# Splitting one projection of eight matmuls around the transposes of the probabilities in a grouped-attention stage

## The reference, cut to what matters

```python
q = _fp8_linear_pertensor(ln_out, wq, wq_scale, q_in_scale).reshape(b, s, g, hpg, d)
q = _ln(q, qln_w, qln_b)
k = _ln(_fp8_linear_pertensor(ln_out, wk, ...).reshape(b, s, g, d), kln_w, kln_b)
v = _fp8_linear_pertensor(ln_out, wv, ...).reshape(b, s, g, d)
core = _gqa(q, k, v).reshape(b, s, nh * d)
qx = _ln(_fp8_linear_pertensor(ln_out, wqx, ...).reshape(b, s, g, hpg, d), qxln_w, qxln_b)
kvx = jnp.einsum('bsi,oi->bso', cond, w_kv_x)
...
xout = _gqa(qx, kx, vx).reshape(b, s, nh * d)
catq = _div_clamp_fp8(jnp.concatenate([core, xout], axis=-1), proj_smooth)
return jnp.einsum('bsi,oi->bso', catq, wproj) * (proj_in_scale * proj_w_scale)
```

## Time and profile before

| what | us |
|---|---|
| median of three runs | 2093.26 |
| lowest and highest | 2092.05, 2093.97 |
| the profiled execution | 2092.42 |
| its span, from the first instruction to the last | 2090.6 |
| TensorE busy in the span | 2021.3 (97%) |
| VectorE, ScalarE, GpSimd busy | 1412.0, 1243.6, 667.7 |
| grouped attention, step 2 to step 58 | 237.1 to 1036.9 in the span |

### The profile page before, as it was taken

How to read it: one execution, slowest core, us unless ns; L and a number is a source line. 1 busy time by engine, 2 the same in 40 slices (tenths; PEclk the granted TensorE clock), 3 DMA queues, 4 the chain that set the end, 5 groups by cost and what they waited for, 6 DMA issues and landing times. The chain is left out here.

```text
span 2090.6 us, 31900 instructions
## 1 busy us (share of the span) xinstructions
PE 2021.3 (97%) x11332; PEld 1579.3 (76%) x11352; DVE 1412.0 (68%) x3113; ACT 1243.6 (59%) x3195; POOL 667.7 (32%) x637
## 2 busy tenths in 40 slices
PE   8999899999999999999998999999999999998998
PEld 5644778888888888888886886665666785666997
DVE  2397576777777777767667747667677658885555
ACT  2073787888787878788774445553554346772332
POOL 1300354444445354535430002324341101222442
PEclk9999999999999999999999999999999999999999
DMA  4033433243424242432222204313322220003200
GB/s 184 22 119 110 134 117 115 73 143 87 146 74 142 87 138 78 128 102 88 92 95 101 76 3 159 132 58 126 116 105 113 86 74 19 2 2 120 107 1 32
DMA packets 60176, 193.71 MB, mean 93 GB/s; under 512 B 9409, under 2 KB 28641, under 8 KB 56049
## 3 DMA queue, kind: packets, MB, share of 16 engines
q1 hardware_dynamic: 48498, 172.16, 24.6%
q10 hardware_dynamic: 9504, 8.50, 1.4%
q0 software_dynamic: 2016, 11.01, 1.3%
HBM read 171.75 MB, written 19.49 MB: 91 GB/s over the span
## 5 line engine op out<-in xcount | busy, mean ns | idle before, releaser
L985 PE MATMUL psum<-la_w_both,context 128*128 128x256 f32 (+1 forms) x1536 | 343.9, 380 | 0.0
L985 PEld LDWEIGHTS psum<-la_w_both,context 128*128 128x128 f32 (+1 forms) x1536 | 277.6, 184 | 44.9
L1456 POOL TENSOR_TENSOR norm_std<-room 128x400 f32<-128x400 f32 x75 | 70.3, 938 | 337.8 <-DVE room L1221 337.7
L942 PE MATMUL psum<-qa_xqf,qa_two 128*128 128x400 f32 x640 | 142.1, 365 | 2.4 <-PEq L60 2.4
L3026 ACT ACTIVATE it_prob<-psum,it_nm 100x257 f32<-100x257 f32 (+1 forms) x256 | 101.9, 413 | 40.0 <-DVE it_nm L3057 39.9
L942 PEld LDWEIGHTS psum<-qa_xqf,qa_two 128*128 128x128 f32 x640 | 119.3, 191 | 7.5 <-issue 3.2
L1003 PE MATMUL psum<-qa_kxT,room 128*100 128x361 f32 x256 | 102.5, 482 | 2.5 <-issue 1.1
L1449 POOL TENSOR_TENSOR room<-room,qa_inv 128x500 f32<-128x500 f32 x64 | 82.1, 1283 | 55.0 <-DMA qa_inv<-qa_std_rows 50.9
L1817 PE MATMUL psum<-gf_parts,gf_w 128*128 128x400 f32 x480 | 93.0, 346 | 0.0
L2565 POOL TENSOR_TENSOR gf_last_diff<-la_gf_what,la_gf_w 128x512 bf16<-128x512 bf16 x24 | 27.0, 1146 | 206.4 <-issue 170.2
L1146 ACT ACT_TABLE_LOAD x64 | 82.1, 1283 | 13.5 <-ACT qa_size L1166 7.1
(11 more groups left out here) (400 smaller groups left out, 5315.5 us busy)
## 6 DMA issues: line engine op xcount, KB each, us to landing
context<-in_context SPq DMA_DIRECT2D x70, 722.0 KB, 5.3
qa_inv<-qa_std_rows SPq DMA_DIRECT2D x64, 250.0 KB, 4.1
qa_w_raw<-in_qa_w SPq DMA_DIRECT2D x8, 1536.0 KB, 16.1
la_gf_raw<-in_gf_w SPq DMA_DIRECT2D x16, 768.0 KB, 4.7
qa_piece<-in_tf_pieces ACTq DMA_DIRECT2D x64, 128.0 KB, 2.1
la_w_qt<-in_qa_o SPq DMA_DIRECT2D x8, 1024.0 KB, 5.5
gf_ternary<-la_gf_made POOLq DMA_DIRECT2D x7, 768.0 KB
gf_ternary<-keep POOLq DMA_DIRECT2D x7, 768.0 KB
```

What stands on the lines that cost most here:

```text
L942: mm = pe.matmul(psum[:, bank, 0:HALF], two[:, part, j, k, :], xqf[:, PART_XQ[j], k, (h % 2) * HALF:(h % 2 + 1) * HALF], start=(k == 0 and ...
L985: mm = pe.matmul(psum[0:rows, i // 2, (i % 2) * 256:(i % 2) * 256 + 256], ctxT[:, n % 2, k, t0:t0 + rows], kv_raw[:, s, k, :], start=(k == ...
```

## The change

In every step from 1 on the `behind` head's eight matmuls are cut in two: the first two chunks of the width (four matmuls) stay ahead of `turn_probs`, the last two (four matmuls) stand behind it. The accumulation in bank 2 of PSUM stays open across the transposes, which write banks 6 and 7. `unit_mm` is raised by the last of the eight, so it comes after the transposes. Step 0 and the `ahead` heads stay as they were. No instruction is added or removed on any engine; VectorE, ScalarE, GpSimd and SyncE keep their order.

```diff
-            def project_unit(u):
+            def project_unit(u, chunks=range(C)):
 
                 h, j = half_and_part(u)
                 bank = bank_of(u)
-                if h >= 2:
-                    pe.wait_ge(S_["w_lo"], (h // 2 - 1) * PARTS + j + 1)
-                if u >= len(FIRST):
-                    pe.wait_ge(S_["raw_ready"], u - 1 if u <= len(FIRST) + 1 else u)
-                for k in range(C):
+                if chunks[0] == 0:
+                    if h >= 2:
+                        pe.wait_ge(S_["w_lo"], (h // 2 - 1) * PARTS + j + 1)
+                    if u >= len(FIRST):
+                        pe.wait_ge(S_["raw_ready"], u - 1 if u <= len(FIRST) + 1 else u)
+                for k in chunks:
                     for part in range(2):
                         mm = pe.matmul(psum[:, bank, 0:HALF], two[:, part, j, k, :],
                                        xqf[:, PART_XQ[j], k, (h % 2) * HALF:(h % 2 + 1) * HALF],
                                        start=(k == 0 and part == 0), stop=(k == C - 1 and part == 1))
-                mm.then_inc(S_["unit_mm"], 1)
+                if chunks[-1] == C - 1:
+                    mm.then_inc(S_["unit_mm"], 1)
...
                 project_context(g, s, b, n)
+                around = n
                 for u in behind(n):
-                    project_unit(u)
+                    project_unit(u, range(C // 2) if around else range(C))
                 if not early(n, 1):
                     turn_probs(n - 1)
+                for u in behind(n) if around else ():
+                    project_unit(u, range(C // 2, C))
                 if not early(n, OUT_LAG):
                     project_out(*out_chunk(g, b, n))
```

## The result

The changed kernel takes 2080.76 us (median of six runs, beside 2093.61 us for the kernel before); the ratio is 0.9941, with a 95% interval of 0.9929 to 0.9952. It is faster by 0.5 to 0.7%. One of its six runs took 2204.71 us at a mean granted clock of 0.927 where the others have 0.991 to 0.994, and one of the six of the kernel before took 2131.85 us; the ratio leaves such slow runs out.

A forecast was written before the change was run, and what follows sets the result against it. TensorE looked saturated but hid short waits at step heads, caused by late transposes. Terms -9.4 - 3.0 + 4.4 + 2.8 - 2.0 = -7.2 us took the median from 2093.26 to 2086.0 us; range 2082 to 2093.5 us.

The forecast's parts named there:

- (a): Steps with n mod 4 = 0 or 1, from 8: earlier transposes give back 0.36 us in 26 steps, -9.4 us.
- The scores need s + 1.53 less two matmuls of 0.18, s + 1.16: Within (a), s being a step's start: earliest start of the scores, reckoned from step 31, which has two more L955 matmuls.
- Their own head gains nothing, as in step 31: Said in (c) of steps with n mod 8 = 3: the start of these steps gets no shorter.
- (c): Steps with n mod 8 = 3, 11 to 51: transposes wait for L1318, +0.73 us in six steps, +4.4 us.
- The chain and its slack: Head chain from the transposes comes 0.71 us earlier; probabilities still in time by 0.13 us after the 0.05.
- Rival 2: ScalarE cannot get ahead, so transposes wait in steps with n mod 8 = 1, 4, 5: 2092.6 us; chance 0.20.
- (b): Steps with n mod 4 = 2, 10 to 58: only 0.23 us ahead of L955 comes back, 13 steps, -3.0 us.
- (d): Steps with n mod 8 = 6: 0.30 us becomes wait, half of 0.23 us lost to GpSimd's L1468; +2.8 us.
- (e): Steps 1, 2, 4, 5, without output projection: matmuls fill L1022's wait, 4 x 0.5 us, -2.0 us.
- Rival 1: VectorE's copy L1221 waits for the raw head's second half: slower, +6.2 us, 2099.5 us; chance 0.10.
- Rival 3: (d) costs nothing because the meeting with L1468 falls out well: -10.0 us, 2083.3 us; chance 0.08.

The follow-up runs named there:

- eight behind: Changed kernel with all eight matmuls of the raw head behind the transposes instead of four: 2102.11 us, ratio 1.0041 to the kernel before.
- late measurement: Changed kernel with ScalarE's measurement of the weights moved behind the exponentials where n mod 8 = 3: 2073.32 us, ratio 0.9905 to the kernel before.

## Why the prediction was right in direction and wrong in size

**What bounds the kernel: right.** TensorE is 97% busy before and after, and yet the stage lost 13.0 us of waits on balance: what it won came at the heads of steps and, in the four early ones, ahead of L1022, and what it paid came ahead of the transposes.

**(a), the term that was mis-sized.** Forecast 0.36 us in 26 steps, measured 0.49: 3.4 of the 5.8 us by which the sum was off. The step that failed is "The scores need s + 1.53 less two matmuls of 0.18, s + 1.16". It took step 31 for a step whose scores wait for nothing. They did wait. In the kernel before, step 31's turned keys end at 646.07 (645.43 and 0.64) and its scores start 0.10 us later, at 646.17, the same distance as in step 36, 715.94 to 716.03:

```profile
645.43 0.64 ACT L1140 ACTIVATE qa_kxT<-psum,params 128x361 f32<-128x361 f32 x1
```

In the changed kernel they end 0.60 us ahead of the scores, which now start at s + 1.45 behind four L957 (638.02 to 639.47):

```profile
638.22 0.65 ACT L1145 ACTIVATE qa_kxT<-psum,params 128x361 f32<-128x361 f32 x1
...
639.47 0.77 PE L1005 MATMUL psum<-qa_kxT,room 128*100 128x361 f32 x2
```

From s + 1.45, two matmuls of 0.18 less give s + 1.09, which is what step 36 does. That is 0.08 of the missing 0.13 us; the other 0.05 us is the longer first pair of a start out of a wait (0.66 and 0.61 us). The run with two matmuls behind has a wait of both parts still in it, and takes 13.3 us.

**"Their own head gains nothing, as in step 31": wrong for the same reason.** Steps with n mod 8 = 7 gained 0.14 us each, 1.0 us, with the same two parts (in step 31 the scores start 0.08 us earlier, and the first pair takes 0.60 us instead of 0.66). In those with n mod 8 = 3 the gain is hidden in the wait of (c).

**The chain and its slack: right.** The turned keys, the low part of the head, the wait of 0.72 us and that of 0.51 us went as foretold. The probabilities were to end 0.18 us ahead of the transposes, 0.13 after the 0.05 of the shortest way. L1323 ends at 715.70, s + 8.47, and the transposes start at 715.83, s + 8.60: 0.13 us, so 0.08 was left. Rival 2, in which they come too late, did not happen in these steps; eight behind shows what it costs when they are late.

**(b): right,** 0.26 us for the 0.23 of the forecast.

**(c): right,** 0.72 us for 0.73. The late measurement then showed whose wait it is: ScalarE's order. The cut only made the transposes reach it 0.73 us earlier.

**(d): too dear by 0.8 us** (with the (b) of the same steps +1.4 forecast, +0.6 measured). The normalisation that met GpSimd's work in the earlier trace rows meets it again and takes the same 1.17 us, but GpSimd's work came earlier too (it ends at s + 9.68 instead of s + 9.98), so that the half that I set down for the meeting was not lost:

```profile
741.93 1.32 POOL L1473 TENSOR_TENSOR qa_v<-qa_w_raw,qa_v 128x512 bf16<-128x512 f32 x1
...
742.15 1.17 DVE L1323 TENSOR_SCALAR qa_prob<-qa_prob,qa_rsum 100x100 f32<-100x100 f32 x1
```

My premise that GpSimd's work stays where it is was wrong. GpSimd is dense from its L1485 to this instruction (L1480 and L1468 before), and ahead of L1485 it waits 0.50 us for VectorE's L1351 (L1346 before). That started at s + 2.68 in the kernel before (744.54) and starts at s + 2.39 in the changed one (735.96), and the whole row came 0.3 us forward in the step. L1323 ends at 743.32, 0.07 us after GpSimd's 743.25, as before (751.91 and 751.84); by the rule of the Trainium skill that I named (SBUF — State Buffer, section "SBUF: two separate sides") that is what a locked port pair looks like, and the trace agrees again. The meeting that did change is another. Of the six steps from 14 on, step 46 took 15.29 us instead of 14.93, in all three executions that have this cut there. There VectorE's clip of the step's outputs (L1346 of the changed kernel) starts 0.05 us behind GpSimd's L1479 and takes 1.48 us; in step 38 it starts 0.17 us ahead of it and takes 0.36 (the instruction behind it on VectorE then takes 1.24):

```profile
734.28 0.36 DVE L1346 TENSOR_SCALAR qa_yb<-la_w_kt 128x400 bf16<-128x400 f32 x1
734.45 1.36 POOL L1479 TENSOR_TENSOR qa_o<-la_w_qt,qa_o 128x512 fp32r<-128x512 f32 x1 [0.77 <-DVE qa_o L1282]
...
844.93 1.29 POOL L1479 TENSOR_TENSOR qa_o<-la_w_qt,qa_o 128x512 fp32r<-128x512 f32 x1 [0.78 <-DVE qa_o L1282]
844.98 1.48 DVE L1346 TENSOR_SCALAR qa_yb<-la_w_kt 128x400 bf16<-128x400 f32 x1
```

What follows on both engines is 0.35 us later in step 46, and so are its transposes. Why the clip starts 0.21 us later there than in the other steps is not shown. Without this one step, (d) was too dear by 1.2 us.

**(e): right in sum,** 2.2 us for 2.0, with some luck: the four steps gave 0.52, 0.74, 0.32 and 0.65 us where I had set down 0.5 for each.

**Rival 1** did not happen. Its cover of 0.15 us was real, and the run with the second half behind the output projection shows the loss behind it, +12.9 us against the kernel before rather than the 6.2 that I gave it; that run delays the head by a whole output projection, which is more than the rival supposed. **Rival 3**, at 2083.3 us, was nearest to the result, but by its (d) alone it explains 0.8 of the 5.8 us.

The range failed with the term: I had put the ends of the unknown costs into (c), (d) and the rivals, and none on (a), since I took its 0.36 us for a measured figure. It was worked out from two steps, and the scores waited in both.

## What to carry to other kernels

Before a step without waits is used as the yardstick for one with waits, look at what releases its own first instructions: here every start of the scores 0.10 us behind the end of ScalarE's keys was a wait, even in step 31, where TensorE was busy for all of its 13.69 us. Where a matmul group has to make room for transposes, count both sides for each kind of step, how much earlier the chain behind the transposes comes and how long the transposes' own operand is already there; here 0.13 us between ready probabilities and their transposes was all that stood between a gain of 0.49 us and a wait. And where the consumer's engine waits while its next operand lies ready, as VectorE did here, changing that engine's order can give most of the gain (here 0.43 of 0.49 us in three of four kinds) without a wait ahead of the transposes.

## What was not expected of the hardware

A start out of a wait costs TensorE more than the wait. The first two matmuls of the scores (L1003, 128x361 f32, one in the code) take 0.66 us up to the first L1004 where they had waited, and 0.61 us in the changed kernel, where they had not; step 31 shows 0.66 and 0.60. The twelve profiled executions agree by kinds of steps: 0.66 us wherever the scores start 0.10 us behind the end of the keys, 0.60 to 0.61 wherever the distance is larger.

The granted clock differs between executions of one program, in places that have nothing to do with the change. The stage won 13.0 us between steps 1 and 60, and the profiled span shows 11.2. Step 1 started 0.5 us later than before, since step 0 began at 207.17 instead of 206.56 (in another execution of the changed kernel at 207.68), and the part behind step 60 took 1.4 us more, though no instruction in it differs. In both profiled executions TensorE had half the full clock (0.50, which is 1.2 GHz) in several short stretches, but not the same ones. The changed kernel had one of 6.8 us just behind the stage, where the kernel before had one of 3.4 us, and one of 3.4 us from 1590.1 on, where the kernel before had none. The window of the first, and that of the kernel before in the same place:

```profile
1095.20:1102.00 6.80, 6.36 (x14) 4.71 (x15) 1.77 (x6) 0.06 (x1) 1.45 (x2) 0.50 0.00 0
...
1107.90:1111.30 3.40, 3.08 (x9) 3.11 (x10) 0.21 (x2) 0.00 (x0) 0.00 (x0) 0.50 0.00 0
```

In the first, eight matmuls of L173 take 4.62 us:

```profile
1098.44 4.62 PE L173 MATMUL psum<-X,avg 128*128 128x400 f32 x8
```

Another profiled execution of the same program gave them 3.00 us, and had the full clock where the second stretch lies:

```profile
1099.54 3.00 PE L173 MATMUL psum<-X,avg 128*128 128x400 f32 x8
```

Over the twelve profiled executions the part behind the start of step 63, the same instructions in all (two of them have one measurement of ScalarE in another place), took from 1002.5 to 1005.6 us: 1005.2 and more in the five with about 20 us at half clock in it, 1004.2 and less in the seven with 10 to 14 us. So up to 3 us of a single span of this kernel say nothing of the change, and a change of that size is to be read from the lengths of its own steps. What decides where the stretches fall no run here shows.
